# An attention pipeline over 32 images: columns formed two images ahead, second statistics used one step later, the spreading of an image's matrices shared by VectorE and GpSimd

## What is computed

```python
# tok: three Haar levels; details weighed by softmax weights of an image, coarse part by a sigmoid; inverse transform
h = tok(x, ...)                                   # (32, 256, 256)
h = concat([cls_tok, h], axis=1)                  # 257 rows an image
e = layernorm(h)
scores = (e @ R) @ e.T + causal_mask              # attention, one image at a time
h = h + softmax(scores) @ e
y = layernorm(h)
# ffn: gate = (tanh(y @ gate_w.T) + 1) / 2; each of 8 experts takes its best 1028 rows of 8224,
#      layernorm, 256 -> 1024 -> gelu -> 256, weighed, added back
h = h + ffn(y)
```

## Time and profile before

| what | value |
|---|---|
| time, median of 3 runs (lowest to highest) | 826.06 us (826.01 to 826.22) |
| time of the profiled execution | 825.02 us |
| its span, first to last instruction | 823.2 us |
| PE busy over the span | 722.4 us, 88% |
| DVE busy | 575.7 us, 70% |
| POOL busy | 462.3 us, 56% |
| ACT busy | 441.4 us, 54% |

### The profile page before, as it was taken

One profiled execution on the slowest core, in us unless ns is written; L12 is line 12 of the kernel. 1 busy time (PEld: TensorE's weight loads), 2 busy tenths in 40 slices (PEclk: granted clock), 3 DMA queues, 4 the chain that ended last, 5 costly groups with the idle time before them and its releaser, 6 DMA issues.

```text
span 823.2 us, 15855 instructions
## 1 busy us (share of the span) xinstructions
PE 722.4 (88%) x4684; PEld 652.6 (79%) x4684; DVE 575.7 (70%) x1902; ACT 441.4 (54%) x971; POOL 462.3 (56%) x680
## 2 busy tenths in 40 slices
PE   6988999999999974845799999999889999999994
PEld 3976777777777763734698999998889999899994
DVE  3674899999999967998776684666736746744441
ACT  1002677777777774102565566656545666556551
POOL 0155587777877754206158557485564674855533
PEclk9989999999999995555999999999979999999997
DMA  9800022122221127301125335243343342433222
GB/s 295 259 1 1 30 77 78 55 73 76 76 76 60 69 81 146 102 0 53 58 41 129 64 65 132 40 107 83 55 123 49 71 124 41 111 77 53 40 26 27
DMA packets 63579, 64.35 MB, mean 78 GB/s; under 512 B 14032, under 2 KB 57104, under 8 KB 63376
## 3 DMA queue, kind: packets, MB, share of 16 engines
q1 hardware_dynamic: 50576, 46.32, 18.1%
q0 software_dynamic: 12800, 17.12, 13.0%
q10 hardware_dynamic: 128, 0.00, 0.0%
HBM read 37.90 MB, written 25.53 MB: 77 GB/s over the span
## 4 chain that ended last, share of the span: by engine, by line
PE 33%; issue 9%; DVE 8%; POOL 6%; ACT 3%; DMA 2%; POOLq 0%; ACTq 0%; DVEq 0%; SPq 0%
PE bank L973 15%; PE bank L987 13%; POOL w2l L515 2%; PE bank L999 2%; POOL out L551 2%; POOL yg L529 2%; DMA raw<-in_fc1T 2%; PE bank L962 2%; ACT bank L713 1%; DVE Tc L1400 1%; DVE yl L1519 1%; PE bank L952 1%; DVE TR L1384 1%; DMA yg<-rows,idx 1%; DVE jk L1496 1%
## 5 line engine op out<-in xcount | busy, mean ns | idle before, releaser
L551 POOL DMA_INDIRECT out<-ob,sidx x72 | 113.9, 1583 | 161.4 <-ACT ob L729 149.7
L1526 DVE TENSOR_TENSOR hl<-bank,hh 128x384 fp32r<-128x384 f32 (+1 forms) x192 | 97.6, 513 | 144.6 <-ACT hh L716 141.2
L713 ACT ACTIVATE bank<-bank,b1s 128x384 f32<-128x384 f32 (+1 forms) x192 | 99.5, 518 | 146.8 <-PE bank L973 142.4
L973 PE MATMUL bank<-yh,w1h 128*128 128x384 f32 (+1 forms) x384 | 133.2, 347 | 10.6 <-DVE hl L1526 3.8
L973 PE MATMUL bank<-yl,w1h 128*128 128x384 f32 (+1 forms) x384 | 123.5, 322 | 2.0 <-issue 2.0
L973 PE MATMUL bank<-yh,w1l 128*128 128x384 f32 (+1 forms) x384 | 124.1, 323 | 0.0
L987 PE MATMUL bank<-w2l,hh 128*128 128x256 f32 x384 | 108.0, 281 | 0.0
L987 PE MATMUL bank<-w2h,hh 128*128 128x256 f32 x384 | 108.0, 281 | 0.0
L987 PE MATMUL bank<-w2h,hl 128*128 128x256 f32 x384 | 107.9, 281 | 0.0
L529 POOL DMA_INDIRECT yg<-rows,idx x72 | 72.4, 1006 | 56.6 <-issue 51.5
L716 ACT ACTIVATE hh<-bank 128x384 fp32r<-128x384 f32 (+1 forms) x192 | 87.7, 457 | 6.1
(11 more groups left out here) (225 smaller groups left out, 1801.1 us busy)
## 6 DMA issues: line engine op xcount, KB each, us to landing
BIG<-in_x SPq DMA_DIRECT2D x4, 2048.0 KB, 14.4
out<-Bs SPq DMA_DIRECT2D x32, 256.0 KB, 2.1
rows<-Yp SPq DMA_DIRECT2D x32, 256.0 KB, 2.3
raw<-in_fc1T SPq DMA_DIRECT2D x16, 512.0 KB
raw<-in_fc2T SPq DMA_DIRECT2D x16, 512.0 KB
yg<-rows,idx POOLq DMA_INDIRECT x72, 2.9
out<-ob,sidx POOLq DMA_INDIRECT x72, 3.8
gwb<-in_gate_w SPq DMA_DIRECT2D x1, 1024.0 KB, 7.2
```

Source lines behind the costliest of these rows:

```text
L551: g.indirect_dma_start(out=out_rows, out_offset=tok(ap=sidx[job.eh][0:m, t:t + 1], axis=0), in_=ob[t % 3][0:m, :], in_offset=None, compute ...
L713: A.activation(h[:, 0:cur.w], h[:, 0:cur.w], ACT.Gelu_apprx_tanh, bias=b1s[:, bass.ds(cur.e, 1), f]).then_inc(s["hact"], 1)
L973: last = T.matmul(Lb[ring(cur, f)][:, 0:cur.w], w1s[cur.eh][i][:, d, f * P:(f + 1) * P], yT[cur.p][k][:, d, 0:cur.w], start=(n == 0), stop ...
L1526: v.tensor_tensor(hT[cur.p][1][:, f, 0:cur.w], Lb[ring(cur, f)][:, 0:cur.w], hT[cur.p][0][:, f, 0:cur.w], ALU.subtract).then_inc(s["hlo"], 1)
```

## The change

`LAG` goes from 4 to 5, so that there are 37 steps and `emit` gets one more image: `e` is t-4, and `m` now is t-5. POOL's steps are run with `ahead` = 2, so that its `nxt` is image t+2. H1 gets four buffers instead of two.

```diff
-        H1 = [sb(f"H1{i}", [P, NH, D]) for i in range(2)]
+        H1 = [sb(f"H1{i}", [P, NH, D]) for i in range(4)]
-        LAG = 4
+        LAG = 5
+        def spread_blocks(ops, m, g0, g1):
+            blocks = OB[:, bass.ds(m.n, 1), g0 * CG:g1 * CG].rearrange("p b (g k) -> p (b g) k", k=CG)
+            wide = [P, g1 - g0, P // CG, CG]
+            return ops.tensor_tensor(OP[m.p][:, g0:g1, :].rearrange("p g (r k) -> p g r k", k=CG),
+                                     blocks.unsqueeze(2).to_broadcast(wide),
+                                     cst("blocks").rearrange("p (r k) -> p r k", k=CG).unsqueeze(1).to_broadcast(wide),
+                                     ALU.mult)
-        def steps(eng, emit):
+        def steps(eng, emit, ahead=1):
-                                       for d in range(1, -LAG - 1, -1)]
+                                       for d in (ahead, *range(0, -LAG - 1, -1))]
...
 # POOL
+            def operators(m):
+                after(po, "z_done", m.n - 1)
+                apart(po)
+                spread_blocks(g, m, 2, 4).then_inc(s["wide_p"], 1)
-                if m:
-                    po.wait_ge(s["u"], m.n + 1)
+                if e:
+                    po.wait_ge(s["u"], e.n + 1)
...
                 if m:
                     po.wait_ge(s["st1"], m.n + 1)
+                after(po, "base", t.n - LAG - 1)
...
+                g.tensor_copy(TST[:, bass.ds(t.n, 1), :].rearrange("p b k -> p (b k)"), st[:, :]).then_inc(s["tab"], 1)
+                if not isinstance(t.n, int) or t.n < NB - 1:
+                    if isinstance(t.n, int) and t.n == HEAD - 1:
+                        po.wait_ge(s["w8"], 2)
+                    operators(t.plus(1))
                 if nxt:
                     columns(nxt)
-                g.tensor_copy(TST[:, bass.ds(t.n, 1), :].rearrange("p b k -> p (b k)"), st[:, :]).then_inc(s["tab"], 1)
...
             columns(Step(0, 0))
+            columns(Step(0, 1))
+            po.wait_ge(s["w8"], 1)
+            operators(Step(0, 0))
             po.wait_ge(s["st_set"], 2)
-            steps(po, emit)
+            steps(po, emit, 2)
...
 # PE
-                    pe.wait_ge(s["wide"], a.n + 1)
+                    for part in ("wide_p", "wide_v"):
+                        pe.wait_ge(s[part], a.n + 1)
...
 # DVE
-                blocks = OB[:, bass.ds(m.n, 1), :].rearrange("p b (g k) -> p (b g) k", g=LEAF)
-                v.tensor_tensor(OP[m.p].rearrange("p g (r k) -> p g r k", k=CG),
...
+                spread_blocks(v, m, 0, 2).then_inc(s["wide_v"], 1)
...
-                if isinstance(t.n, int) and t.n == EARLY + 5:
+                if isinstance(t.n, int) and t.n == EARLY + 6:
...
-                    after(dve, "tab", t.n)
-                    v.reciprocal(ST[1 - t.p][:, 14:16], rsm[d.p][:, :]).then_inc(s["rv"], 1)
+                    dve.wait_ge(s["tab"], t.n + 1)
+                    v.reciprocal(st[:, 14:16], rsm[d.p][:, :]).then_inc(s["rv"], 1)
...
-                    after(dve, "base", d.n - 1)
+                    after(dve, "base", d.n - 3)
...
-                        last = v.bn_aggr(ST[1 - t.p][:, 4 + 2 * h:6 + 2 * h], bn1[:, h, :])
+                        last = v.bn_aggr(st[:, 4 + 2 * h:6 + 2 * h], bn1[:, h, :])
```

More of the change, by code:

```diff
@@ L206, in build_program @@
         TEG = sb("TEG", [P, NB, NH, NE])
-        TST = sb("TST", [P, NB + 4, 16])
+        TST = sb("TST", [P, NB + 5, 16])
         LM = sb("LM", [CG * NJ, NB, CG])
@@ L618, in base_rows, with emit @@
                     after(act, f"base_st{m.p}", m.h * 16)
-                half = A.activation(Bs[m.p][:, h, :], H1[m.p][:, h, :], ACT.Identity,
-                                    bias=N6[m.p][:, 2 + h:3 + h], scale=O1[m.p][:, h:h + 1])
+                half = A.activation(Bs[m.p][:, h, :], H1[m.r][:, h, :], ACT.Identity,
+                                    bias=N6[1 - m.p][:, 2 + h:3 + h], scale=O1[1 - m.p][:, h:h + 1])
                 if h == 1:
                     half.then_inc(s["base"], 1)
-            def emit(t, _nxt, _a, b, c, d, m):
-                if isinstance(t.n, int) and t.n == EARLY + 7:
+            def emit(t, _nxt, _a, b, c, d, _e, m):
+                if isinstance(t.n, int) and t.n == EARLY + 8:
                     act.wait_ge(s["gt_c"], 6)
@@ L674, in emit @@
                     for h in range(NH):
-                        last = A.activation(Yp[m.p][:, h, :], H1[m.p][:, h, :], ACT.Identity,
+                        last = A.activation(Yp[m.p][:, h, :], H1[m.r][:, h, :], ACT.Identity,
                                             bias=N6[t.p][:, 4 + h:5 + h], scale=ST[t.p][:, 12 + h:13 + h])
@@ L1271, in emit @@
                     gate_terms(0, EARLY, 0)
-                if isinstance(t.n, int) and t.n == EARLY + 6:
+                if isinstance(t.n, int) and t.n == EARLY + 7:
                     gate_sums(0, EARLY, 0)
                     gate_scaled(0, EARLY, 0)
-                if isinstance(t.n, int) and t.n == EARLY + 7:
+                if isinstance(t.n, int) and t.n == EARLY + 8:
                     gate_values(0, EARLY, 1)
@@ L1312, in emit @@
                 if d:
-                    st_next = ST[1 - t.p]
                     dve.wait_ge(s["av"], d.n + 1)
@@ L1324, in emit @@
                     for h in range(NH):
-                        last = v.scalar_tensor_tensor(out=H1[d.p][:, h, :], in0=U[d.p][:, h, 0:D],
-                                                      scalar=st_next[:, 14 + h:15 + h], in1=hc[d.r][:, h, :],
+                        last = v.scalar_tensor_tensor(out=H1[d.r][:, h, :], in0=U[d.p][:, h, 0:D],
+                                                      scalar=st[:, 14 + h:15 + h], in1=hc[d.r][:, h, :],
                                                       op0=ALU.mult, op1=ALU.add)
@@ L1341, in emit @@
                     for h in range(NH):
-                        last = v.bn_stats(bn1[:, h, :], H1[d.p][:, h, :])
+                        last = v.bn_stats(bn1[:, h, :], H1[d.r][:, h, :])
                     last.then_inc(s["st1_b"], 1)
```

17 lines of the change are left out of this document (8 added, 9 removed).

## The result

The changed kernel takes **811.56 us** in the median of 6 runs (809.85 to 813.48), the kernel before 826.03 beside it (6 runs, 824.18 to 826.49): ratio 0.9839, interval 0.9822 to 0.9855. It is faster, clear of the noise though by less than 2%, and by 14.5 us in the medians, twice the 7.0 that were forecast (819.0); the time lies outside the range (813.5 to 826.0). Ratios and their 95% intervals are those on record; they aren't simply the quotient of the two medians beside them. The profiled execution took 813.24 us, one of the longer of the six, of which 811.4 are the span; before it was 825.02 and 823.2.

What follows compares the result with a forecast made beforehand. Neither DVE nor PE alone but a ring through POOL, with POOL-DVE meetings, was taken to bound the step. 26 x (7.325 - 6.98) = 9.0 us less, 2.0 more at the end: 826.06 becomes 819.0 us, range 813.5 to 826.0.

Steps and rivals of the forecast that it cites:

- Everything behind it shifts as a block: Behind the last image (rows of image 31, Tanh, gate values, search, experts): all moves together, own times unchanged, 0 us.
- Ring: DVE's last work, POOL's scales and columns, PE's inverse transform, DVE's next step: with meetings, makes steps 7.325; change cuts it.
- the 0.34 us that I read as DVE's wait for PE: DVE between L1348 and L1283: 0.50 us where it waited, 0.16 otherwise; the 0.34 would go.
- Step of 6.98: DVE's step after the change: 6.54 + 0.24 + 0.2 = 6.98 us, above PE's 6.82.
- DVE's half at 0.42 + 0.2: DVE's half of the spreading: 0.42 us for 128 x 256, plus 0.2 for meeting POOL's half or L458.
- L1325's loss: DVE's pair L1325, held up by POOL's columns: 0.24 us a step kept, between 0 and 0.35.
- POOL's half: POOL's 128 x 256 part of the shared spreading: about 0.6 us more in POOL's step.
- DVE gains 0.27: Sharing the spreading cuts DVE's L1247 from 0.69 to 0.42 us, 0.27 a step.
- Fill: The start-up steps before 95.28 us: gain or lose up to 0.5 us, taken as 0.
- End, +2.0: Two sets of POOL's scales after the last TUG copy instead of one: +2.0 us, between 1.2 and 2.9.
- Slack of the reciprocal: DVE's reciprocal newly waits for POOL's table copy: slack 0.8 us, so no cost unless POOL comes late.
- Rival 1: PE sets the step at 6.82 us as DVE's operations slip between POOL's: 815.0 us; chance 0.15.

Runs made afterwards that it cites:

- before_pe11: The kernel before with 22 always-fulfilled waits (11 instructions) added on PE behind the last image: 819.34 us, ratio 0.9917.
- after_pool24: The changed kernel with 24 more instructions (always-fulfilled waits) on POOL ahead of the first gather: 810.23 us, ratio 0.9804.
- after_no_xc: The changed kernel without PE's wait for the columns, PE's stream again 2866 instructions ahead of the expert loop: 819.35 us, ratio 0.9920.
- no_share: The changed kernel with DVE spreading all four groups and POOL none, PE's stream filled up to 2877 instructions: 808.08 us, ratio 0.9809.
- no_share_end: no_share with POOL's last TUG copy (image 31, step 35) put behind that step's scales: 807.83 us.

## Why the prediction was wrong

**The step that failed** is the sentence "Everything behind it shifts as a block". It took it that code which the change leaves alone takes the same time. PE's 11 new waits moved the loop over experts in PE's instruction stream and took away a stall that is worth about 6 us, and the new place of POOL's code made the first gather late, which cost 2.85 us. The rows were there to be read: two stops of PE in a row with no believable releaser. I never looked past the search. With the code of PE and POOL where both are free of these, the change is worth 9.1 us (before_pe11 819.34, after_pool24 810.23, side by side), for a forecast of 7.0; in their profiles image 1 comes 2.2 us earlier, which the forecast had at 0. That after_no_xc stands 6.6 us under before (0.9920), near my 7.0, is luck: it has before's stall and the late gather as well.

Point by point:
- *Ring*: right, PE's and DVE's waits are gone and POOL waits for L1356. The part that cut it is the second statistics; the columns add 0.03 us a step. But the 0.34 us that I read as DVE's wait for PE was read in the step with the loop's jump back, where it stays. And more came from the H1 pair, 0.25 us a step, than from the waits.
- *Step of 6.98*: 7.003 measured. DVE's half at 0.42 + 0.2 = 0.62: 0.60. L1325's loss, 0.24: 0.26. POOL's half: 0.73 for 0.6.
- *"DVE gains 0.27"*: right as a term and wrong as an account of what sharing is worth. I kept L1325's loss (0.24) in both cases; in truth it goes when POOL starts earlier (pair at 0.492 each in no_share) and comes back with POOL's half (0.621). Sharing gains 0.16 and costs 0.26. The Trainium skill's rule of the exclusive lock (SBUF — State Buffer, section "SBUF: two separate sides") spoke against sharing, and the runs agree with it, but I had let it raise the price of one meeting only, not look for a new one.
- *Fill, "I take 0"*: -3.4 in this pair of profiles, the second error in size. The columns bring about 2 of it. (In before_pe11, which is before in this stretch, image 1 comes at 94.05, so some 0.7 can be scatter.)
- *End, +2.0*: +1.81 behind image 31. Ahead of it, 1.4 more in the last step, where the clock fell in this execution, less 0.7 in the three shorter steps before it.
- *Slack of the reciprocal*: right, no wait for the table from 100 to 260 us. At the end, where DVE's list gets shorter, there are three (2.19 us at 282 and at 289 us, 0.50 at 296), in steps of 6.6 us that are shorter than the 7.0 before them, but for the last.
- *Rival 1* (PE at 6.82) could not have been: PE goes below it. *Rival 2* needed 0.77 us of meetings a step; it had 0.26 on the pair and 0.18 on the half.

In the sum two misses had one sign, -3.4 and -5.5, and the late gather (+2.85) stood against them, with 1.2 from the steps and the end. They make the 4.8 us between the profiles' 11.8 and my 7.0. The other 2.7 lie between profiles and medians: before's profile is 1.0 under its median, the changed kernel's 1.7 over.

## What to carry to other kernels

An edit that adds or removes a few instructions on an engine moves every loop behind it in that engine's stream, and here that was worth about 6 us beside the 9.1 of the change itself. Before a gain or a loss is put down to an edit, compare the packets of the instruction queues and look at the first instructions behind each loop's jump back; a few idle waits put the code where it was. And take work from a busy engine only if the engine that gets it has a place where it meets nothing: look at what it pushes, not only at what it takes by itself.

## What the hardware showed that I had not expected

- The jump back of a loop on PE cost nothing or about 6 us (3.70 and 1.98 of standing, the rest at the lower clock), by 11 instructions ahead of it.
- The first gather after 33 to 35 us of waiting came 1.1 us behind its index or 3.4, by 24 instructions ahead of it. That the fetch does it is likely, not shown: the instruction queues' packets stay the same.
- The clock fell behind a wait of PE of 2.16 us in one execution and not in another of the same code (7 of the 16 profiles that have this wait, with 0.9 to 1.8 us more in the last step).
- Every fourth DVE step, the one with the loop's jump back, takes 0.6 us longer in no_share (7.4 for 6.8): 0.34 us of it lies between two instructions with no releaser but "issue", and the rest is a spreading that meets POOL (0.99 for 0.69).
- Operations of POOL of 128 x 2 and 128 x 4 (0.19 to 0.23 us alone) took 0.41 to 0.60 us under DVE's sums over the gates, operations with two SBUF inputs of 0.6 us (end of no_share_end).
